# Two of four PSUM evictions of the quantized transpose moved from VectorE to ScalarE

## The reference

```python
xn  = layernorm(x)
# branch s (a rank-8 recurrence and a rank-32 feed-forward)
xm  = layernorm(xn) * gamma + beta
u   = xm @ W_in + b_in                      # [.., 8]
h   = scan(h[t] = sigmoid(decay_logit) * h[t-1] + u[t])
x2  = xn + h @ W_out + b_out + xm * D_skip
hf  = relu((layernorm(x2) * gamma + beta) @ W_down + b_down)   # [.., 32]
s   = x2 + hf @ W_up + b_up
# branch g (a 2048 x 2048 product of 8-bit-quantized operands)
y   = relu(fake_quant(xn) @ fake_quant(kernel) + fake_quant(bias))
g   = silu(fake_quant(y))
out = x + s * g
```

## Time and profile before

| | |
|---|---|
| time, median of 2 runs | 2313.55 us (2313.34 to 2313.75) |
| time of the profiled execution | 2312.74 us |
| its span on the slowest core | 2311.2 us |
| spans of the 8 cores | 2310.1 to 2311.2 us |
| granted TensorE clock, mean | 0.739 |

### The profile page before, as it was taken

One profiled execution on the slowest core, in us unless ns is written; L12 is line 12 of the kernel. 1 busy time (PEld: TensorE's weight loads), 2 busy tenths in 40 slices (PEclk: granted clock), 3 DMA queues, 4 the chain that ended last, 5 costly groups with the idle time before them and its releaser, 6 DMA issues.

```text
span 2311.2 us, 26987 instructions; the slowest of 8 cores (2310.1 to 2311.2 us)
## 1 busy us (share of the span) xinstructions
PE 1380.5 (60%) x5025; PEld 608.9 (26%) x5025; DVE 1154.1 (50%) x2855; ACT 671.1 (29%) x740; POOL 298.7 (13%) x132
## 2 busy tenths in 40 slices
PE   0434343356666666666666666666666666666664
PEld 0222222222222222222222222222222222222221
DVE  4333333355555555555555555555555555555553
ACT  0111211213333333333333333333333333333332
POOL 0000000001111111111111111111111111111111
PEclk9999999996676666676666666666666666666666
DMA  1112112101111111111111111111111111111110
GB/s 20 50 37 52 40 39 53 55 0 37 37 37 37 37 37 37 37 37 37 37 37 37 37 37 37 37 37 37 37 37 38 37 37 37 37 37 43 40 37 28
DMA packets 56491, 86.47 MB, mean 37 GB/s; under 512 B 11118, under 2 KB 44014, under 8 KB 52206
## 3 DMA queue, kind: packets, MB, share of 16 engines
q1 hardware_dynamic: 56348, 84.75, 14.7%
HBM read 51.17 MB, written 33.55 MB: 37 GB/s over the span
## 4 chain that ended last, share of the span: by engine, by line
DVE 36%; PE 29%; issue 16%; ACT 12%; POOL 3%; DVEq 2%; SPq 1%; ACTq 0%; DMA 0%; POOLq 0%
PE py L702 13%; DVE x L605 4%; DVE x2tmp L604 4%; POOL s L789 3%; PE pb L409 3%; PE pb L375 3%; DVE st L472 3%; PE pb L566 3%; ACT xn L468 3%; DVE s L680 3%; DVE t L449 3%; DVEq L73 2%; DVE u_sb L574 2%; DVE kstat L384 2%; ACT g L784 2%
## 5 line engine op out<-in xcount | busy, mean ns | idle before, releaser
L702 PE MATMUL py<-kq,ixqT 128*128 128x512 bf16 x2048 | 587.0, 458 | 39.2 <-DVE x L605 31.3
L789 POOL TENSOR_TENSOR s<-g,s 128x1024 f32<-128x1024 f32 x64 | 150.1, 2346 | 1991.2 <-ACT g L784 1895.6
L702 PEld LDWEIGHTS py<-kq,ixqT 128*128 128x128 bf16 x2048 | 231.8, 114 | 403.4 <-issue 252.6
L510 PE MATMUL pb<-eyef,xn 128*128 128x128 f32 x512 | 137.7, 373 | 189.7 <-DVE xnT L514 146.6
L629 ACT ACTIVATE sqscr<-x 128x512 f32<-128x512 f32 x128 | 80.6, 630 | 414.0 <-DVE x L605 412.7
L456 ACT ACTIVATE st<-nw 128x2 f32<-128x2 f32 x32 | 6.6, 205 | 573.2 <-DVE nw L455 573.2
L793 POOL TENSOR_TENSOR o<-s,x 128x1024 f32<-128x1024 f32 x64 | 149.7, 2340 | 17.5 <-POOL s L789 17.5
L510 PEld LDWEIGHTS pb<-eyef,xn 128*128 128x128 f32 x512 | 82.4, 161 | 251.1 <-issue 223.9
L527 PE MATMUL pb<-eyeb,qbf 128*128 128x128 bf16 x512 | 125.8, 265 | 10.1 <-ACT qbf L482 1.6
L412 DVE CAST kq<-pb 128x512 bf16<-128x512 f32 x64 | 44.3, 692 | 161.0 <-PE pb L409 161.0
L472 DVE TENSOR_REDUCE st<-xn 128x1 f32<-128x2048 f32 x32 | 73.1, 2286 | 78.6 <-ACT xn L468 78.6
(11 more groups left out here) (173 smaller groups left out, 1811.4 us busy)
## 6 DMA issues: line engine op xcount, KB each, us to landing
x<-L_attn_x SPq DMA_DIRECT2D x32, 1024.0 KB, 8.5
out<-o SPq DMA_DIRECT2D x64, 512.0 KB, 3.5
xn<-L_ffn_kernel SPq DMA_DIRECT2D x128, 64.0 KB, 2.3
s<-L_ffn_kernel SPq DMA_DIRECT2D x128, 64.0 KB, 2.1
wint<-L_attn_W_in SPq DMA_DIRECT2D x16, 4.0 KB
wdnt<-L_attn_W_down SPq DMA_DIRECT2D x16, 16.0 KB
x<-L_attn_W_up SPq DMA_DIRECT2D x1, 256.0 KB
eyef<-c_eye_f SPq DMA_DIRECT2D x1, 64.0 KB
```

Of the source, the lines that this page charges most:

```text
L510: tlast = T(deps, lambda e, j=j, b=b, bank=bank, xn=xn: e.transpose(bank[:, 128 * b:128 * (b + 1)], xn[:, 128 * j:128 * (j + 1)], eyef[:]) ...
L702: mmlast = T(deps, lambda e, j=j, qq=qq, fofs=fofs, ixb=ixb: e.matmul(py[qq][:], ixb[:, 128 * j:128 * (j + 1)], kq[:, D * j + fofs:D * j + ...
L789: sg = G([e4, rc["s1"], rc.get("tap_s")], lambda e, h=h: e.tensor_tensor(sb_[:, 1024 * h:1024 * (h + 1)], g_t[:], sb_[:, 1024 * h:1024 * ( ...
```

## The change

For the two later groups (g = 2 and 3) of the quantized transpose, the copy from PSUM to ixqT is issued on ScalarE as an activation with the identity function, in place of VectorE's tensor_copy. It stands at the same place of the written order, inside emit_mid. Data, buffers and dependencies are unchanged, but what depends on these two copies (t2e[2], t2e[3]) now waits for ScalarE's semaphore: the L702 matmuls of blocks 8 to 15, the four L597, the first L668 and the first L510 of the next chunk.

```diff
-                t2e.append(V([tlast, dep_ix_free],
-                             lambda e, g=g, ixb=ixb, bank=bank: e.tensor_copy(ixb[:, 512 * g:512 * (g + 1)], bank[:])))
+                if g < 2:
+                    t2e.append(V([tlast, dep_ix_free],
+                                 lambda e, g=g, ixb=ixb, bank=bank: e.tensor_copy(ixb[:, 512 * g:512 * (g + 1)], bank[:])))
+                else:
+                    t2e.append(S([tlast, dep_ix_free],
+                                 lambda e, g=g, ixb=ixb, bank=bank: e.activation(ixb[:, 512 * g:512 * (g + 1)], bank[:], AF.Identity, bias=0.0, scale=1.0)))
```

## The result

The changed kernel takes 2327.33 us (median of 38 runs), the kernel before 2314.22 us (37 runs), and the ratio of the two is 1.0049 with a 95% interval of 1.0039 to 1.0059. It is slower by 9 to 14 us, well inside 2%. The forecast was 2317.2 us: no visible change, a range of 2308 to 2332. The range held and the class was right. Of the 13 us that were lost, the forecast had 3.7.

The account below looks back on a forecast made before the run. It took a serial chain through each of 32 chunks as the bound, no engine near full. Per chunk 0.05 + 0.06 = 0.11 us, 3.4 over 31, plus 0.3 for the first, 3.7 on 2312.74, plus 0.8: 2317.2 us, range 2308 to 2332.

Parts of the forecast that it names:

- The stall as cover: L574 waits for GpSimd's L793, giving 1.06 us mean slack per chunk against L546's 1.08 us delay; overshoot taken as 0.05.
- Rival A: The stall at L574 does not cover the delay; 1.08 to 1.26 us per chunk count, 2347 to 2353 us; chance 9%.
- The evictions' price: Two ScalarE activations between second silu and L546 make L546 1.04 to 1.26 us later; 1.08 taken, from L629.
- Rival B: Activations out of PSUM take much longer than from SBUF; at 1.3 us each, 48 us lost, 2361 us; chance 3%.
- VectorE's relief: Two L531 casts of 0.69 us per chunk leave VectorE, which idles 2.55 us until L549; gain on the path 0.
- Rival C: The boundary waits for VectorE, so 1.38 us per chunk is saved, 43 us, time 2270 us; chance 2%.
- The price of a wait: One more wait in TensorE's queue costs 0.10 us of issue; at L597 0.06 us per chunk taken, at worst 0.40.
- L702 and L668: Extra waits on half the L702 matmuls and one L668 cost 0: issue is ahead, and L668's reader stands behind L719 and L722.
- rival D: TensorE issue becomes the bound through waits at L702, L597 and L668: 1.3 us per chunk, 40 us, 2354 us; chance 4%.
- The clock: Where the clock rises within an L702 half may shift the mean period: 9 us either way, put into the range only.

Follow-up runs that it names:

- E5: Kernel before, with GpSimd's last operation of a chunk (L793, second half) adding 64 columns in place of 1024; 2272.7 us, run once.
- E6: Changed kernel with GpSimd's last operation of a chunk cut to 64 columns in place of 1024; cores at clock 0.738 to 0.740 have 2314.8 to 2318.8 us.
- E3: Against the kernel before, only the third eviction (g = 2) moved to ScalarE, the fourth left on VectorE; ratio 1.0018.
- E1: Changed kernel, wait for the moved fourth eviction kept only on the first of a chunk's four L597 matmuls; timed again 2314.39 us, ratio 1.0001.
- E4: Changed kernel, with only the first L702 matmul of each group of blocks 8 to 15 keeping one wait, the others none; ratio 1.0075.
- E2: Kernel before with nothing moved, each L597 matmul given one more wait, on the long finished L546 copy of ScalarE; ratio 1.0058.
- E7: Kernel before, leaving out every wait whose value the same engine has already waited for on the same semaphore; ratio 0.9777.
- F1: Kernel before, with the small addition of L574 (8x128) done by ScalarE in place of VectorE; 2298.76 us, ratio 0.9937.
- F3: Kernel before without repeated waits and with the small addition of L574 on ScalarE; 2236.15 us, ratio 0.9678.

## Why the prediction was right, and where it fell short

**The stall as cover: right.** L546 is 0.95 us late (1.04 to 1.26 forecast, 1.08 taken), the stall shrinks by 0.92 us on average, and L578 still ends 0.07 us behind GpSimd. E5 and E6 show the cause and E3 the proportion. What overshoots the cover is 0.03 us per chunk, by the repeated run of E1 (15.32 us from silu to big matmul against 15.28); the forecast took 0.05. Rival A, without this cover, would have been 2347 to 2353 us.

**The evictions' price: right, a little high.** 584 ns against 630 of the same shape out of SBUF, and (1346.12 - 1345.16)/2 = 0.48 us from start to start. The Trainium skill (Perfetto Trace Analysis, Optimizing Scalar/DVE Operations) puts ScalarE's overhead at about 93 ns on SBUF and 51 on PSUM, 42 ns lower, and the estimate from it was 0.98 us of delay, nearer to the measured 0.95 than the value taken. That the recorded durations here differ by 46 ns confirms it only loosely: the two operations differ in function and output type as well, and by the same page a recorded duration holds about twice the overhead. Rival B, evictions of 1.27 us, has fallen.

**VectorE's relief: right.** It was worth nothing. Rival C has fallen: VectorE's busy time fell by 74 us, and with the waits taken out (E1 run again) the time is that of the kernel before, not less.

**The price of a wait: right; its place: wrong.** The step "I take 0.02 for each of three, 0.06; at worst 4 x 0.10 = 0.40" is where the forecast missed. Per chunk the term measured 0.30 us, the whole 0.10 at each of three. The step said that L597's output is ready 0.24 us before its reader starts and that 0.14 would do, since "VectorE is seen to start 0.09 behind the end of the TensorE work it waited for (L543 1336.76, L531 1336.85)". But that L531 reads what the L527 matmuls wrote, and L543 merely came last ahead of it: the 0.09 is no handover. The line's own record in the kernel before says so:

```profile
L531 DVE CAST ixqT<-pb x128: 691/692/693, 484.8 to 2246.4; 128x512 bf16<-128x512 f32 x128
its engine sat idle before it (us, times) until:
  PE pb L527: 43.7, 125
  PE pff L543: 0.7, 1
```

In the other 31 chunks the last L531 starts before L543 has ended, and the chunk shown is the one exception. The gap of 0.24 us was itself the time of the handover, since with the wait added it is still 0.25 and everything has moved. Slack of an operation is to be read from a pair that does wait for one another. Rows of this kind were at hand, L604 itself, four times per chunk.

With 0.30 in place of 0.06 the sum would have been 2312.74 + 31 x 0.35 + 0.3 = 2323.9, and with the 0.8 between that execution and the median 2324.7, within 3 us of what was measured.

**L702 and L668: right.** For L702 E4 and the unchanged 0.21 us per load show it; L668 has no run of its own, but with the waits of L597 alone taken out (E1 run again) no loss is left for it. Of rival D the L597 term, 0.4, was nearly true at 0.3, and its other terms measured nothing.

**The clock: inside the allowance of 9 us either way.** At an equal granted clock of 0.739 the changed kernel's cores average 2320.9 us over its runs and the kernel before's 2310.5 in the runs beside E1's repetition: 10.4 us, about the 31 x 0.32 of the traces. The other 3 us of the 13 go with the slowest cores, at 0.737 in place of 0.739. In the profiled execution the slowest core lost 0.10 us per chunk between the first big matmul and the next second silu (41.64 us on average against 41.55 before), where core 1, at 0.740, lost none (41.50). That this comes from where the clock rises within a big half is argued from these figures; no run separates it, but E1's repetition shows that it goes when the waits go.

## What to carry to other kernels

A full queue is not a path: what decides is what each follower waits for last, and a stall on another engine can swallow a whole added operation, until someone removes the stall. Moving work to another engine moves its semaphore too, and each consumer may gain a wait instruction of 0.10 us, which counts where it is issued behind the wait that ends last; look for consumers in tight back-and-forth loops between two engines, and keep a wait only where it is the first of its value on that engine. Take the slack ahead of a reader from a pair that does wait for one another.

## What the runs showed of the hardware that was not expected

- A wait instruction whose condition is long met costs 0.10 us of TensorE's issue (E2: steps of 1.77 in place of 1.66 us; 0.106 us between the two waits in the changed kernel's trace). Where TensorE's issue is ahead of its matmuls it costs nothing (E4). Leaving out 7,504 instructions of the kernel before gave 2.2% (E7).
- How long after a matmul's recorded end its reader on VectorE starts depends on the matmul: 0.24 to 0.25 us for L597 (2x512), 0.11 for L527 and L569, 0.17 for L548 (medians in the kernel before).
- The scan on VectorE (8x128, both inputs in SBUF) is held by a running GpSimd tensor_tensor as the tensor_scalar is: 0.99 us in F1 and 1.38 in F3, against 0.47. By the Trainium skill (SBUF — State Buffer, Who interferes with whom) a VectorE instruction with two inputs in SBUF contends with a GpSimd instruction that reads SBUF; F1 agrees with its 0.99 us.
